# Four transformer layers on one core: row blocks of the sorted experts fetched in another order, a table part computed earlier, POOL drained twice more

## The chip, the core and the metric

The kernel is one program on one core of a Trainium2 chip. The core has five engines with instruction queues of their own: PE (TensorE, matmuls), DVE (VectorE), ACT (ScalarE), POOL (GpSimd) and SP (SyncE, which here only issues DMAs). They meet through semaphores. Times are device microseconds of one execution. Three executions of the kernel before took 1379.13, 1385.40 and 1386.09 us, median 1385.4 us. A fourth one was profiled.

## The reference

The input is `L0_attn_x`, 8 x 512 x 128 in fp32, which is 4096 tokens of 128 numbers. Four layers follow, each a pre-norm attention and a pre-norm feed-forward part:

```
x = L0_attn_x
x = x + _L0_attn_ref(_layernorm(x), ...)   # causal, no softmax, 16 heads of 8
x = x + _L0_ffn_ref(_layernorm(x), ...)    # one of 4 groups of 2 experts (128 -> 256 -> 128, silu gate)
x = x + _L1_attn_ref(_layernorm(x), ...)   # linear attention, elu + 1
x = x + _L1_ffn_ref(_layernorm(x), ...)    # one of 8 experts (128 -> 512 -> 128, relu), at most 512 tokens each
x = x + _L2_attn_ref(_layernorm(x), ...)   # sliding window of 64, softmax
x = x + _L2_ffn_ref(_layernorm(x), ...)    # dense, 128 -> 384 -> 128, int weights
x = x + _L3_attn_ref(_layernorm(x), ...)   # latent attention with rope, pages
x = x + _L3_ffn_ref(_layernorm(x), ...)    # one of 8 experts (128 -> 512 -> 128, exact gelu), no limit
return x
```

What matters here is that layers 0 and 3 route each token to one expert (group) by an argmax, and that the number of tokens of an expert is known only at run time. In layer 3:

```
expert_idx = jnp.argmax(router_probs, axis=-1)
h = jax.nn.gelu(x_flat @ w1[e] + b1[e], approximate=False)
y = h @ w2[e] + b2[e]
out = out + jnp.where(sel, expert_w, 0.0)[:, None] * y
```

## The kernel before, in words

The activations stay in SBUF (`X`, 32 tiles of 128 tokens). The program has six stretches, with a barrier of all five engines between any two. A barrier is a semaphore `bar` that every engine raises once; PE, DVE, ACT and SP raise it with a DRAIN instruction, POOL with a small memset of `mark` (line 2037), and each then waits for five more. Inside a stretch the order of each engine's work is fixed beforehand: by `lanes` from tables of due times (`ORDER0`, `ORDER2`) or written out by hand (`ORDER1`).

The first stretch is the attention and the routing of layer 0. While it runs, POOL scatters every token with an indirect DMA (line 2101) into a DRAM table `xs0`, sorted by expert: expert g owns 4096 rows. At its end DVE computes from the counts (`tables0`) a table `row_at` of 19 slots: for each slot the row of `xs0` at which 256 tokens of one expert begin, and the row of the weights. Then comes the barrier, and after it the first sorted expert stage: a slot s is fetched by SP (`fetch_x`, 132 KB, and `fetch_w`, 768 KB, into rings of four buffers), turned on PE (`g0_turn`, line 755), copied by ACT, multiplied up (`g0_up`, lines 767 and 768), activated, multiplied down (line 780), and POOL scatters the result back (`put`, line 2127). `g0_turn(1)` waits until ACT has copied the result of `g0_turn(0)`, and `g0_up(0)` stands behind both turns in PE's queue.

The row numbers are loaded by SP into a register (`slot_row`, a TENSOR_LOAD at line 2206), some register instructions make an address of it, and only then the DMA is issued (line 2218 for rows, 2212 for weights). The first weights are fetched ahead of the barrier (`grouped_ahead`), the first rows may not be: the last tokens are scattered just before it. `W_NEXT` says which weights follow which rows: in layer 0 the weights of slot s + 1 stand behind the rows of slot s, for s below 3.

Layer 3 has the same form with 23 slots of 256 or 128 tokens (`PLAN3`): three pairs of slots that share their weights, ten slots of 256 and seven of 128. Its table is made in parts by `tables3(level)`: level 4 ahead of the barrier (the first three pairs), level 2 behind it, and level 1 after the first rows have been turned. Each part raises `tab`, for which SP waits before it uses a row number of that part. DVE also copies the turned rows (line 1721), in the same queue as the table. In this stage POOL's `put` adds the result to `out` in DRAM with an indirect DMA (line 2127): one for each 128 tokens, so 39 for the 23 slots. POOL issues 205 indirect DMAs in the whole program (96 + 38 + 32 + 39). After the last it waits until all have landed, and the program's end follows, where every engine executes one more DRAIN (line 2331).

PE ends the first stretch with `warm(8)`, eight matmuls whose result nobody reads, then raises its barrier, and runs `warm(4)` behind it; the stretch before the last stage does the same with `warm(6)`.

The lines that decide most of it:

```
def barrier():                                   # SP's, line 2182
    S.drain().then_inc(sem["bar"], 1)
    e.wait_ge(sem["bar"], 5 * bars)

def fetch(L, s):                                 # line 2230
    if s > 3:
        e.wait_ge(sem["g_tok"], SLOT0[L] + s - 3)
    fetch_x(L, s)
    if L == 3 and s in TAB3:
        e.wait_ge(sem["tab"], TAB3[s])
    for n in W_NEXT[L].get(s, []):
        fetch_w(L, n)
```

Of the kernel before, what the change touches and what calls it, by code (L numbers as in the profile page):

```python
# [131 lines left out]
TILES3, COL3, WNUM3 = plan3()  # L132
SLOTS = {0: 19, 3: len(TILES3)}
# [5 lines left out]

W_NEXT = {0: {s: [s + 1 if s < 3 else s] for s in range(SLOTS[0]) if s != 3}, 3: {1: [1], 2: [2], 3: [3]}}  # L140
for n in range(4, len(PLAN3)):
    W_NEXT[3].setdefault(max(last_use3(n - 4) + 4, 4), []).append(n)
TAB3 = {1: 3, 2: 4}
# [218 lines left out]
def build(nc, inp, out):  # L362
    with ExitStack() as ctx:
# [217 lines left out]
        def pe_program(e):  # L581
# [9 lines left out]
            def warm(n):  # L591
                for _ in range(n):
                    PE.matmul(ps[:, 7, :], ident, W[:, 0:512], start=True, stop=True, skip_group_check=True)
# [152 lines left out]
            e.wait_ge(drained_of(last[:2], last[2]), after(last[:2], last[2]))  # L746
            warm(8)
            barrier()
# [340 lines left out]
        def dve_program(e):  # L1089
# [258 lines left out]
            def tables3(level):  # L1348
# [51 lines left out]
                if level == 4:  # L1400
# [19 lines left out]
                    choose(0, FOURS, 512)  # L1420
                if level == 2:
                    own.end(V.scalar_tensor_tensor(out=got, in0=take, scalar=512.0, in1=base, op0=ALU.mult, op1=ALU.add))
                    own.end(V.tensor_tensor(out=odd, in0=til, in1=full, op=ALU.subtract))
                    own.end(V.scalar_tensor_tensor(out=four, in0=take, scalar=-2.0, in1=full, op0=ALU.mult, op1=ALU.add))
                    settled()
                    limited(four, PAIRS)
                    scan(f(504), odd)
                    settled()
# [223 lines left out]
            for name, b in ORDER2["DVE"]:  # L1652
# [53 lines left out]
                elif name[:2] == "l3":  # L1706
                    tail(3, name, b)
            tables3(4)
            barrier()
            tables3(2)  # L1710
# [318 lines left out]
        def pool_program(e):  # L2029
# [140 lines left out]
            ysb3 = gviews(3)[4]  # L2170
            e.wait_ge(sem["out_done"], 16 * (B + 3))
            for s in range(SLOTS[3]):
                put(SLOT0[3] + s, s % 4, out, ysb3[s % 4], ALU.add, TILES3[s])
            for s in range(SLOTS[3], SLOTS[3] + 4):
# [3 lines left out]
        def sp_program(e):  # L2178
            e = Seat(e)
            bars = 0  # L2180

            def barrier():
                nonlocal bars
                bars += 1
                S.drain().then_inc(sem["bar"], 1)
                e.wait_ge(sem["bar"], 5 * bars)

            def stack(key, l):
# [24 lines left out]

            def fetch_x(L, s):
                k, E = s % 4, 4 if L == 0 else 8
                u = 2 if L == 0 else TILES3[s]
                rows = xs[L][bass.ds(slot_row(0, s if L == 0 else COL3[s], E * 4096), 128 * u), :].rearrange("(p u) d -> p u d", u=u)
                S.dma_start(gviews(L)[2][k][:, 0:u, :], rows).then_inc(gx[k], 16)
# [47 lines left out]
            e.wait_ge(sem["y1_rows"], 48)  # L2266
            barrier()
            for name, b in ORDER1["SP"]:
                if name == "g0_f":
                    fetch(0, b)  # L2270
                elif name == "f2":
                    S.dma_start(f2.bitcast(I32), inp["l2_ffn"]).then_inc(sem["f2_in"], 16)
                elif name == "l1_get":
                    due = min(2 * (b + 1) + 3, SLOTS[0])
                    for k in range(4):
                        e.wait_ge(y_out[k], 32 * len(range(k, due, 4)))
                    e.wait_ge(sem["mixed"], b)
                    S.dma_start(yg1, ys[0][1 + T * b:1 + T * b + T, :].rearrange("(t p) d -> p t d", p=128)).then_inc(sem["y0_in"], 16)
                elif name == "w1":
                    e.wait_ge(sem["g_down"], SLOTS[0])  # L2280
                    S.dma_start(MW[:, 512 * b:512 * b + 512], inp["l1_moe"][:, 512 * b:512 * b + 512]).then_inc(sem["w1_in"], 16)
# [44 lines left out]
            grouped_ahead(3)  # L2326
            barrier()
            for s in range(SLOTS[3]):
                fetch(3, s)
# [142 lines left out]
```

## Time and profile before

| what | value |
|---|---|
| three executions | 1379.13, 1385.40, 1386.09 us (median 1385.4) |
| profiled execution, its own time | 1376.14 us |
| its span (first to last instruction) | 1374.2 us |
| busy in the span: PE, DVE, ACT, POOL | 1102.5, 823.4, 568.4, 446.0 us |
| mean granted clock of PE | 0.927 |
| barrier ahead of the first sorted stage | about 202.4 us |
| barrier ahead of the last sorted stage | about 1270.4 us |
| last busy instruction of any compute engine ends | about 1365.9 us |

The profiled execution's own time is 1.9 us above its span. A row of the trace names an engine, the line of the kernel, the tile that it writes and those that it reads, and how often it stands there. A name with a q (SPq, POOLq, PEldq) is the engine's own instruction queue: register, semaphore, drain and DMA-issuing instructions, which count as no busy time. In a timeline, brackets give how long the engine had been idle before the instruction and who ended that.

### The profile page before, as it was taken

How to read it: one execution, taken by the hardware profiler on the slowest of the kernel's cores; microseconds unless marked ns; L12 is line 12 of the kernel's file. 1: busy time of each engine (PE TensorE's matmuls, PEld its weight loads, DVE VectorE, ACT ScalarE, POOL GpSimd, SP SyncE). 2: the span in 40 equal slices, each digit the busy share in tenths (PEclk: the TensorE clock that was granted, in tenths of full speed). 3: DMA queues.
4: the chain of work that ended last, by engine and by line, in shares of the span. 5: the costliest groups of instructions: out<-in, count | busy, mean ns of one | idle time of the engine just before them, and what ended most of it. 6: DMA issues, size and time to landing. Idle time of an engine off the chain costs nothing.

```text
span 1374.2 us, 39349 instructions
## 1 busy us (share of the span) xinstructions
PE 1102.5 (80%) x16861; PEld 803.4 (58%) x16861; DVE 823.4 (60%) x2399; ACT 568.4 (41%) x993; POOL 446.0 (32%) x538
## 2 busy tenths in 40 slices
PE   6999968888976794676788988888888887766895
PEld 4777747777864473443455655656565564443784
DVE  7577765568875122346748587686848575734432
ACT  3322103455451231314374654737374552551342
POOL 3223331344564154113122223133321403112475
PEclk9999979999996997788999999999999999877998
DMA  9454415543040511212211211212221100200784
GB/s 363 166 204 187 178 59 182 169 140 116 25 160 22 121 51 51 52 48 55 54 51 50 67 50 37 63 46 58 60 58 49 48 25 11 55 18 27 192 212 91
DMA packets 85167, 126.15 MB, mean 92 GB/s; under 512 B 14465, under 2 KB 66178, under 8 KB 84578
## 3 DMA queue, kind: packets, MB, share of 16 engines
q1 hardware_dynamic: 68258, 106.57, 24.6%
q0 software_dynamic: 10928, 13.64, 4.1%
q10 hardware_dynamic: 5808, 3.43, 0.9%
q8 instruction: 132, 2.16, 0.7%
q14 instruction: 41, 0.34, 0.1%
HBM read 50.92 MB, written 46.74 MB: 71 GB/s over the span
## 4 chain that ended last, share of the span: by engine, by line
PE 38%; DVE 26%; ACT 10%; issue 10%; POOL 7%; DMA 5%; SPq 1%; another core or an unknown queue 1%; PEldq 1%; ACTq 1%; DVEq 0%; PEld 0%; POOLq 0%
DVE mx L1680 10%; ACT MW L1963 5%; DVE mx L1671 2%; DVE bst L1112 2%; PE ps L873 2%; PE ps L1033 2%; PE ps L976 2%; PE ps L858 2%; PE ps L780 2%; PE ps L967 2%; POOL xs L2101 2%; PE ps L889 2%; PE ps L767 1%; PE ps L768 1%; DVE X L1140 1%
## 5 line engine op out<-in xcount | busy, mean ns | idle before, releaser
L1680 DVE TENSOR_REDUCE mx<-ps 128x2 f32<-128x1024 f32 (+3 forms) x176 | 188.4, 1119 | 33.2 <-PE ps L1006 33.0
L1963 ACT ACTIVATE MW<-ps 128x1024 f32<-128x1024 f32 x160 | 154.6, 1029 | 75.9 <-PE ps L1018 62.9
L2101 POOL DMA_INDIRECT xs<-xr,sidu x96 | 96.2, 1002 | 138.8 <-DVE sidu L1271 101.3
L2044 POOL TENSOR_SCALAR rst<-bmv 128x4 f32<-128x4 f32 x64 | 15.8, 246 | 286.6 <-DVE bmv L1115 285.9
L1033 PE MATMUL ps<-MW,Vp 128*16 128x128 f32 x2560 | 88.2, 279 | 3.7 <-ACT MW L1963 3.5
L1006 PE MATMUL ps<-K,Q 64*128 64x512 bf16 (+3 forms) x512 | 61.6, 315 | 22.9 <-DVE mx L1680 16.9
L1950 ACT ACTIVATE MW<-ps 128x1024 f32<-128x1024 f32 x64 | 63.6, 1030 | 25.3 <-PE ps L938 23.3
L601 PE MATMUL ps<-W,xr 128*128 128x128 f32 x192 | 36.6, 323 | 45.5 <-DVE xr L1125 32.5
L1033 PEld LDWEIGHTS ps<-MW,Vp 128*16 128x16 f32 x2560 | 64.1, 98 | 15.2 <-ACT MW L1963 4.6
L2127 POOL DMA_INDIRECT out_dram<-qf,toku x39 | 60.6, 1555 | 34.9 <-DVE toku L1736 26.7
L1769 ACT COPY XT<-ps 128x512 f32<-128x512 f32 x48 | 28.2, 588 | 101.2 <-PE ps L601 83.2
L1671 DVE TENSOR_REDUCE mx<-ps 128x8 f32<-128x768 f32 x64 | 57.9, 949 | 18.7 <-PE ps L915 16.3
L1018 PE MATMUL ps<-Q,K 64*128 64x128 bf16 x1280 | 58.9, 222 | 9.9 <-DMA Q<-mT 3.9
L2023 ACT ACTIVATE MW<-ps,MW 128x256 f32<-128x256 f32 (+1 forms) x92 | 34.0, 439 | 60.3 <-PE ps L1078 58.1
L1018 PEld LDWEIGHTS ps<-Q,K 64*128 64x128 bf16 x1280 | 39.0, 96 | 31.2 <-issue 12.2
L601 PEld LDWEIGHTS ps<-W,xr 128*128 128x128 f32 x192 | 25.8, 168 | 52.3 <-issue 32.1
L1112 DVE BATCH_NORM_STATS2 bst<-X 128x6 f32<-128x128 f32 x256 | 55.4, 278 | 1.2
L2127 POOL DMA_INDIRECT ys<-xp,toku x38 | 37.6, 990 | 55.7 <-DVE toku L1524 46.9
L1006 PEld LDWEIGHTS ps<-K,Q 64*128 64x128 bf16 x512 | 19.2, 95 | 55.0 <-DVE mx L1680 26.4
L634 PE MATMUL ps<-W,tmpA 128*128 128x128 f32 x256 | 41.0, 288 | 12.8 <-DVE mx L1680 4.4
L2047 POOL TENSOR_TENSOR rst<-rst,npow 128x4 f32<-128x4 f32 x48 | 49.8, 1038 | 4.0
L1140 DVE TENSOR_TENSOR X<-ps,X 128x512 f32<-128x512 f32 x40 | 27.6, 690 | 36.4 <-PE ps L739 10.7
(373 smaller groups left out, 2675.2 us busy)
## 6 DMA issues: line engine op xcount, KB each, us to landing
xs<-hb SPq DMA_DIRECT2D x52, 528.0 KB, 9.1
MW<-l_moe_dram SPq DMA_DIRECT2D x19, 768.0 KB
MW<-l_moe_dram SPq DMA_DIRECT2D x20, 578.0 KB
Q<-spl SPq DMA_DIRECT2D x48, 128.0 KB
Q<-spm SPq DMA_DIRECT2D x48, 128.0 KB
K<-spl SPq DMA_DIRECT2D x43, 128.0 KB
K<-spm SPq DMA_DIRECT2D x43, 128.0 KB
MW<-l_moe_dram SPq DMA_DIRECT2D x16, 256.0 KB
```

Source lines behind the costliest of these rows:

```text
L601: m = PE.transpose(p[:, 128 * t:128 * t + 128], xr_of(key)[:, t, 0:128], ident)
L1006: m = PE.matmul(p[:, o:o + nk], Q3[i][64 * k:64 * k + 64, s, 128 * t:nk], K3[i][64 * k:64 * k + 64, s, 0:nk], start=True, stop=True, tile_ ...
L1018: m = PE.matmul(p[:, o:o + 128], K3[i][64 * k:64 * k + 64, 4 * half + s, 128 * kt:128 * kt + 128], Q3[i][64 * k:64 * k + 64, 4 * half + s, ...
L1033: m = PE.matmul(ps[32 * j:32 * j + 16, 7, 128 * g:128 * g + 128], Vp[1][:, 4 * i + kt, h, :], P3[k % 2][:, col(h)[0] + 128 * col(h)[1]:col ...
L1112: own.end(V.bn_stats(out=bst[:, k, t, :], in_=X[:, 4 * b + t, :]))
L1671: V.tensor_reduce(out=mx[0][:, :, 4 * half:4 * half + 4, t], in_=p.rearrange("p (e n) -> p e n", e=2)[:, :, 0:384].rearrange("p e (s k) -> ...
L1680: V.tensor_reduce(out=mx[1][:, :, s0:s0 + ns, t], in_=p.rearrange("p (e n) -> p e n", e=2)[:, :, 0:ns * nk].rearrange("p e (s k) -> p e s ...
L1950: A.activation(P2[t % 2][:, 1024 * half:1024 * half + 1024], p, ACT.Exp).then_inc(drained[u], 1)
L1963: A.activation(P3[k % 2][:, 1024 * half:1024 * half + 1024], p, ACT.Exp).then_inc(drained[u], 1)
L2047: G.tensor_tensor(out=rst[:, k, 1, :], in0=rst[:, k, 0, :], in1=npow[:, :], op=ALU.pow).then_inc(rstd_on[k], 1)
L2101: G.indirect_dma_start(out=xs[L], out_offset=bass.IndirectOffsetOnAxis(ap=sidu[:, 4 * b + t:4 * b + t + 1], axis=0), in_=src[:, t, :], in_ ...
L2127: G.indirect_dma_start(out=dst, out_offset=at, in_=y[:, v, :], in_offset=None, compute_op=how).then_inc(y_out[k], 16)
```

## The change

Four things are changed.

First, SP at the two barriers. The barrier is split into `arrive` (the DRAIN) and `passed` (the wait). Between the two SP loads the row numbers of slots 0 and 1 into registers. Behind the barrier it issues the rows of slots 0 and 1, and after them the weights of slot 1. In layer 0 these weights used to stand between the two row blocks; in layer 3 the two row blocks already stood first, but each with its own load ahead of it.

Second, DVE: the first thirteen instructions of the old level 2 (through `limited(four, PAIRS)`) are now `tables3(3)` and stand ahead of the barrier. The rest of level 2 stays behind it.

Third, PE: `warm(8)` becomes `warm(6)` at the end of the first stretch.

Fourth, POOL: a DRAIN stands ahead of the 23 puts of the last stage, and another one ahead of the put of slot 11. By then POOL has issued 166 indirect DMAs before the first DRAIN, 19 more before the second, and 20 follow.

```
-W_NEXT = {0: {s: [s + 1 if s < 3 else s] for s in range(SLOTS[0]) if s != 3}, 3: {1: [1], 2: [2], 3: [3]}}
+W_NEXT = {0: {s: [s] for s in range(4, SLOTS[0])}, 3: {1: [1], 2: [2], 3: [3]}}
...
-            warm(8)
+            warm(6)
             barrier()
             warm(4)
...
-                if level == 2:
+                if level == 3:
                     own.end(V.scalar_tensor_tensor(out=got, in0=take, scalar=512.0, in1=base, op0=ALU.mult, op1=ALU.add))
                     own.end(V.tensor_tensor(out=odd, in0=til, in1=full, op=ALU.subtract))
                     own.end(V.scalar_tensor_tensor(out=four, in0=take, scalar=-2.0, in1=full, op0=ALU.mult, op1=ALU.add))
                     settled()
                     limited(four, PAIRS)
+                if level == 2:
                     scan(f(504), odd)
...
             tables3(4)
+            tables3(3)
             barrier()
             tables3(2)
...
             e.wait_ge(sem["out_done"], 16 * (B + 3))
+            G.drain()
             for s in range(SLOTS[3]):
+                if s == SLOTS[3] // 2:
+                    G.drain()
                 put(SLOT0[3] + s, s % 4, out, ysb3[s % 4], ALU.add, TILES3[s])
...
-            def barrier():
+            def arrive():
                 nonlocal bars
                 bars += 1
                 S.drain().then_inc(sem["bar"], 1)
+
+            def passed():
                 e.wait_ge(sem["bar"], 5 * bars)
...
+            def x_row(L, s):
+                return slot_row(0, s if L == 0 else COL3[s], (4 if L == 0 else 8) * 4096)
...
-            barrier()
+            arrive()
+            first = [x_row(0, s) for s in range(2)]
+            passed()
+            for s in range(2):
+                fetch_x(0, s, first[s])
+            fetch_w(0, 1)
+            for s in (2, 3):
+                fetch_x(0, s)
+                fetch_w(0, s)
             for name, b in ORDER1["SP"]:
                 if name == "g0_f":
-                    fetch(0, b)
+                    if b > 3:
+                        fetch(0, b)
...
             grouped_ahead(3)
-            barrier()
-            for s in range(SLOTS[3]):
+            arrive()
+            first = [x_row(3, s) for s in range(2)]
+            passed()
+            for s in range(2):
+                fetch_x(3, s, first[s])
+            e.wait_ge(sem["tab"], TAB3[1])
+            fetch_w(3, 1)
+            for s in range(2, SLOTS[3]):
                 fetch(3, s)
```

The order of SP's instructions at the first sorted stage, before. `MW` is the weights' ring, `tco` the rows' ring, a TENSOR_LOAD fetches one number of `row_at`, an ISA row is register work. The barrier stands between the first DMA and the load behind it; drains and waits are not shown.

```order
L2212 DMA MW<-l0_moe_dram 128x1536
L2206 TENSOR_LOAD row_at
L2218 ISA
L2218 DMA tco<-xs0 128x264
L2206 TENSOR_LOAD row_at
L2212 ISA
L2212 DMA MW<-l0_moe_dram 128x1536
L2206 TENSOR_LOAD row_at
L2218 ISA
L2218 DMA tco<-xs0 128x264
```

And the same place now:

```order
L2223 DMA MW<-l0_moe_dram 128x1536
L2217 TENSOR_LOAD row_at x2
L2233 ISA
L2233 DMA tco<-xs0 128x264
L2233 ISA
L2233 DMA tco<-xs0 128x264
L2217 TENSOR_LOAD row_at
L2223 ISA
L2223 DMA MW<-l0_moe_dram 128x1536
```

The second row block has moved from behind the weights of slot 1 to before them, and both of the first loads now stand directly behind the first weights.

PE's queue around the first barrier, as the difference of the two programs:

```order
 L626 MATMUL ps<-hota,W 128x16
-L593 MATMUL ps<-W 128x512 x12
+L593 MATMUL ps<-W 128x512 x10
 L755 MATMUL ps<-W,tco 128x128 x4
```

Only the two unread matmuls are gone (eight and four before, six and four now); the turns of the first rows follow as before. DVE's instructions have the same order in both programs; what moves there is the place of the barrier among them.

## Rows read from the trace of the kernel before

**Rows 1.** Busy time by window: the last sorted stage (us, engines, PEclk, DMA share, GB/s)

```profile
1272.00:1366.00 94.00, 79.31 (x540) 70.26 (x539) 35.41 (x156) 33.99 (x92) 60.64 (x39) 0.99 0.75 178
```

**Rows 2.** Instructions of line 2331, the program's end (ns min/median/max, first and last start)

```profile
L2331 POOLq COMPARE_BRANCH  x1: 41/41/41, 1367.6 to 1367.6; - x1
L2331 POOLq DRAIN  x1: 6196/6196/6196, 1367.8 to 1367.8; - x1
```

**Rows 3.** DMA traffic from 1367.8 us to the end

```profile
DMA packets 0, 0.00 MB, mean 0 GB/s; under 512 B 0, under 2 KB 0, under 8 KB 0
```

**Rows 4.** Instructions of line 2462, the program's start

```profile
L2462 POOLq DRAIN  x1: 169/169/169, 0.3 to 0.3; - x1
```

**Rows 5.** Groups by line: POOL's indirect DMAs (count, busy us, mean ns, idle before)

```profile
L2101 POOL DMA_INDIRECT xs<-xr,sidu x96 | 96.2, 1002 | 138.8 <-DVE sidu L1271 101.3 <-issue 24.4 <-DVE sidu L1265 13.1
...
L2127 POOL DMA_INDIRECT out_dram<-qf,toku x39 | 60.6, 1555 | 34.9 <-DVE toku L1736 26.7 <-issue 8.2
...
L2127 POOL DMA_INDIRECT ys<-xp,toku x38 | 37.6, 990 | 55.7 <-DVE toku L1524 46.9 <-issue 8.9
...
L2145 POOL DMA_INDIRECT ys<-qf,gidu x32 | 30.6, 958 | 49.3 <-DVE qf L1612 41.6 <-issue 7.6
```

**Rows 6.** Timeline of POOL, last stage (start, us, line, operation, idle before and releaser)

```profile
1284.99 1.62 POOL L2127 DMA_INDIRECT out_dram<-qf,toku  x1 [14.61 <-DVE toku L1736]
...
1324.23 1.55 POOL L2127 DMA_INDIRECT out_dram<-qf,toku  x1 [1.41 <-DVE toku L1736]
...
1335.65 1.55 POOL L2127 DMA_INDIRECT out_dram<-qf,toku  x1 [2.21 <-DVE toku L1736]
...
1356.93 1.55 POOL L2127 DMA_INDIRECT out_dram<-qf,toku  x1 [2.46 <-DVE toku L1736]
...
1364.36 1.55 POOL L2127 DMA_INDIRECT out_dram<-qf,toku  x1 [0.30 <-issue]
```

**Rows 7.** Chain that ended last, around the first sorted stage's barrier (start, us, what)

```profile
193.33 9.02 PEldq L588
202.37 0.28 SPq L2206
```

**Rows 8.** Waits of SP's queue (total us, times, longest)

```profile
SPq L2206 <- PEq L588: 0.5, 1, 0.5
```

**Rows 9.** Timeline of all engines, start of the first sorted stage

```profile
201.28 0.36 SPq L2212 DMA_DIRECT2D MW<-l_moe_dram  x1
...
202.81 0.35 SPq L2218 DMA_DIRECT2D tco<-xs  x1
...
204.43 0.33 SPq L2218 DMA_DIRECT2D tco<-xs  x1
...
206.76 0.44 PE L755 MATMUL ps<-W,tco 128*128 128x128 f32 x2 [0.67 <-DMA tco<-xs]
...
207.30 0.37 ACT L1839 COPY tco<-ps 128x256 f32<-128x256 f32 x1 [18.41 <-PE ps L755]
...
209.48 0.44 PE L755 MATMUL ps<-W,tco 128*128 128x128 f32 x2 [2.28 <-DMA tco<-xs]
```

**Rows 10.** Busy time by window: the first transfers of that stage

```profile
202.00:205.25 3.25, 3.17 (x8) 1.42 (x8) 1.98 (x5) 0.00 (x0) 0.00 (x0) 1.00 0.87 289
202.00:208.20 6.20, 4.46 (x11) 1.65 (x10) 1.98 (x5) 0.37 (x1) 0.00 (x0) 1.00 0.89 300
```

**Rows 11.** Timeline of all engines, start of the last sorted stage

```profile
1268.66 0.17 DVE L1382 TENSOR_SCALAR row_at<-tab 128x3 int32<-128x3 f32 x1
...
1270.42 0.17 DVE L1422 SCALAR_TENSOR_TENSOR rt<-rt 128x8 f32<-128x8 f32 x1 [1.59 <-POOL mark L2037]
...
1271.61 0.17 DVE L1386 TENSOR_TENSOR_SCAN rt<-rt 128x8 f32<-128x8 f32 x1
...
1274.08 0.44 PE L1054 MATMUL ps<-W,tmpA 128*128 128x128 f32 x2
...
1275.48 0.42 DVE L1721 COPY tmpA<-ps 128x256 f32<-128x256 f32 x1
```

More of the change, by code:

```diff
@@ L2185, in barrier @@
                 S.drain().then_inc(sem["bar"], 1)
+            def passed():
                 e.wait_ge(sem["bar"], 5 * bars)
+            def barrier():
+                arrive()
+                passed()
             def stack(key, l):
@@ L2212, in fetch_w, with fetch_x @@
                 S.dma_start(gviews(L)[0][k], src[bass.ds(slot_row(1, s if L == 0 else COL3[WNUM3.index(s)], 128 * E - 128), 128), :]).then_inc(gw[k], 16)
-            def fetch_x(L, s):
-                k, E = s % 4, 4 if L == 0 else 8
+            def x_row(L, s):
+                return slot_row(0, s if L == 0 else COL3[s], (4 if L == 0 else 8) * 4096)
+            def fetch_x(L, s, row=None):
+                k = s % 4
                 u = 2 if L == 0 else TILES3[s]
-                rows = xs[L][bass.ds(slot_row(0, s if L == 0 else COL3[s], E * 4096), 128 * u), :].rearrange("(p u) d -> p u d", u=u)
+                row = x_row(L, s) if row is None else row
+                rows = xs[L][bass.ds(row, 128 * u), :].rearrange("(p u) d -> p u d", u=u)
                 S.dma_start(gviews(L)[2][k][:, 0:u, :], rows).then_inc(gx[k], 16)
@@ L2326, in sp_program @@
             grouped_ahead(3)
-            barrier()
-            for s in range(SLOTS[3]):
+            arrive()
+            first = [x_row(3, s) for s in range(2)]
+            passed()
+            for s in range(2):
[3 more added lines that the diff above has]
+            for s in range(2, SLOTS[3]):
                 fetch(3, s)
```

## The prediction

> **What bounds the kernel now.** I read the views in the order end, stage, start. The end first: the last POOL instruction starts at 1364.36 and takes 1.55 us [rows 6], so all compute is over at 1365.91, but the span ends at 1374.2. Of these 8.3 us the instructions of the program's last line show where they go: POOL's queue passes its waits for the last landings by 1367.65, and then a single DRAIN of POOL takes 6.196 us [rows 2]. In those 6.2 us no DMA packet moves at all [rows 3]. So the last 0.45% of the time is one queue instruction that shows in no list of busy groups. The only other DRAIN of POOL stands at the start, when it has issued no DMA, and takes 0.169 us [rows 4]. Between the two POOL has issued 96 + 39 + 38 + 32 = 205 indirect DMAs [rows 5].
>
> Then the stage ahead of the end. POOL's puts run at 1.55 us with 0.30 between them, but the reader is to see in the timeline that POOL waits for DVE's `toku` again and again, the last time 2.46 us before the final five [rows 6]. So the stage is paced by the chain PE, DVE, SP and the weights' DMA, not by POOL; a late POOL in the middle is caught up.
>
> Then the two starts. At the first barrier the chain goes through PE's own queue, 9.02 us of drain behind the unread matmuls, and then to SP's load [rows 7]; yet SP waited only 0.5 us for PE [rows 8]. Behind it PE turns the first rows at 206.76 and the second only at 209.48, after 2.28 us of waiting for `tco`, and the first product stands behind that turn [rows 9]. At the last stage's barrier DVE sits idle 1.59 us until POOL's mark, then computes the table from 1270.42 on, and copies the turned rows at 1275.48 although PE had turned them from 1274.08 to 1274.52 [rows 11]. There DVE's table is the bound, not the rows.
>
> Everything between the two places is a chain of waits of one engine for another that starts from the first barrier, with nothing tied to the clock on the wall. So time gained at 202 us is carried to the end.
>
> **The last DRAIN.** Taken as a fixed 0.169 us plus an equal share for each DMA issued since the last DRAIN, 6.196 - 0.169 over 205 is 29.4 ns each. With a DRAIN at 166 and one at 185, the last one finds 20: 0.169 + 20 x 0.0294 = 0.76 us. Saving 5.4 us. The bounds: nothing saved if the time has nothing to do with the count, 6.0 us if it falls to the 0.169 us of the start. I take 5.4, since the two DRAINs in the trace differ in just this, the DMAs issued before them, and no transfer was left to wait for.
>
> The Trainium skill speaks against it: "VectorE: DVE Perf Modes", section "The DRAIN you can't avoid", says that the DRAINs of preamble and postamble cost a constant of about 12 ns on all five engines. By that rule the sum would be the 2.65 us of the starts alone. The trace differs, 6196 ns for POOL's last one.
>
> **The DRAIN ahead of the puts.** By the same rate 166 DMAs cost 0.169 + 4.9 = 5.1 us. It starts when the barrier opens at 1270.4, and POOL has nothing to do until 1284.99, an idle time of 14.61 us [rows 6]. It costs nothing up to 14 us, with the old 6.2 us too.
>
> **The DRAIN at slot 11.** Nineteen DMAs of the stage stand before it, the 20th is the one at 1324.23 [rows 6]. The DRAIN has to wait until the 19th has landed: from the end of the last DMA's issue to the end of POOL's waits is 1367.65 - 1365.91 = 1.7 us, and 0.169 + 19 x 0.0294 = 0.7 us come behind it. That is 2.4 us, of which the idle 1.41 less the usual 0.30 covers 1.1. The 20th put is 1.3 us late at most. The gaps at 1335.65 and 1356.93 give back 2.21 + 2.46 - 0.60 = 4.07 us, so nothing is left of it at the end. What queues behind it is only POOL's own puts; DVE needs their output buffers again four slots later, some 10 us on. Cost 0; bounds 0 and, if this DRAIN took the whole 6.2 us behind the landing, 1.7 + 6.2 - 1.1 - 4.07 = 2.7 us.
>
> **First sorted stage.** SP arrives at the barrier at 202.37 - 0.5 = 201.87. Taking away two of PE's eight unread matmuls from a piece of 9.02 us shortens it by more than 0.5 us even at twice the mean pace, so the barrier opens with SP at about 201.9; no more than 0.5 us can come from it. SP's two loads take 0.28 each [rows 7] with about 0.03 between, register work 0.15, so the rows of slot 0 are issued at about 202.6 instead of 202.81, those of slot 1 at about 203.0 instead of 204.43. But the rows of slot 0 do not come sooner: they stand behind 768 KB of weights issued at 201.28, and from 202.00 to 205.25 at 289 GB/s 0.94 MB moved, which is just these weights and the 132 KB [rows 10]. The turn of slot 1 waited for 1.86 MB (6.2 us at 300 GB/s: two weights and two row blocks [rows 10]), done at 208.2, and PE started 1.3 us later. Now it waits for 1.06 MB, done at about 205.7, there at about 207.0. The next limit is late at once: `g0_turn(1)` also waits for ACT's copy, which ends at 207.67 [rows 9]. So it starts at 207.7 instead of 209.48: 1.8 us. Bounds: 0 if the transfers share the engines and slot 1's rows come no sooner; 2.3 if slot 0's rows too come by the 0.5 us of the barrier. The second weights are issued at about 203.8 instead of 203.6, and by the measured rate are done at 208.2 and usable at 209.5; only if `g0_up(0)`, which starts at 208.1, took less than 1.4 us for its eight products of 128 x 256 would PE wait for them.
>
> The removed unread matmuls leave PE idle for about 1.3 us at the barrier. The granted clock stays at 1.00 until 208.2 [rows 10], well into the 2.28 us of idle before 209.48 [rows 9], which is the 2.4 GHz level, so I charge nothing.
>
> **Last sorted stage.** The thirteen moved instructions take from 1270.42 to 1271.61, 1.19 us [rows 11]. DVE's last instruction before the barrier ends at 1268.83 and it then idles 1.59 us, so they fit with 0.4 us to spare, less DVE's own DRAIN. The table then ends 1.19 us sooner, at 1274.3 instead of 1275.5, but the copy now has to wait for PE's turn, over at 1274.52. It starts at about 1274.6 instead of 1275.48: 0.88 us. SP's two loads begin only when it arrives, close to the barrier itself, so its rows are 0.1 us later at worst. I take 0.85 us; bounds 0 and 1.19. The second copy stands behind the rest of the table, as before, and keeps the shift.
>
> The skill has a figure against this: "DMA: Bandwidth & Descriptors", section "Latency and other measured facts", gives a TENSOR_LOAD a floor of about 600 ns. Two of them would put the rows 0.6 us later, and this stage would keep 0.2 us. Row 202.37 shows 0.28 us.
>
> **Sum.** 5.4 + 1.8 + 0.85 = 8.05 us. Against the profiled execution's own 1376.14 us that is 1368.1. The median of the three runs is 9.3 us above that execution, so the same saving stands against 1385.4: 1377.3 us, forecast 1377.
>
> **Rivals.**
> Not shortened: the last DRAIN keeps its 6.2 us, because it is a fixed price of a POOL that has issued indirect DMAs. Then each added one costs the same. The one at slot 11 leaves 2.7 us at the end, and 2.65 come from the starts: 0.05 us in all, 1385 us. For it: there is only one long DRAIN, so no rate can be read from it. Against: nothing that POOL or the DMAs do is left at 1367.8.
>
> Starts given back: slot 1's rows come no sooner, or PE falls to its lower clock at the first barrier, and only 5.4 + 0.85 = 6.25 us remain: 1379 us. For it: the transfers stand at 0.87 to 0.89 of all engines [rows 10]. Against: the row blocks of slot 0 did come when 0.94 MB had moved.
>
> Slower: the DRAIN at slot 11 waits for a moment in which no DMA at all is in flight, SP's weights too. They keep the DMA engines at a share of 0.75 through the stage [rows 1], and stop only when DVE stops, in slot 15, because the buffers of slot 11 are not free, so that SP's last fetch is the one released by slot 14, whose put is at 1335.65 [rows 6]: near 1336.5. With 3.3 us for the last weights (592 KB at this stage's 178 GB/s) the DRAIN ends near 1340, and the 20th put is 16 us late; less 4.07 that is 12 us at the end, against 8.05 gained: 4 us slower, 1389 us. It decides from a hold of POOL of 8.05 + 4.07 = 12.1 us on. Against: the last DRAIN ran 6.2 us with nothing in flight, so it wasn't packets that it waited for.
>
> **Chances.** Forecast 0.73, not shortened 0.14, starts given back 0.09, slower 0.04. About 0.5% or 6.9 us is what a measurement of this kernel can tell from no change; the three runs themselves lie 7 us apart. The forecast's 8.05 is only 1.1 us above that line, and medians of runs that spread like this move by some 2 to 3 us, so I give it two chances in three of showing as faster, the third case one in three: 0.73 x 0.67 + 0.09 x 0.33 = 0.52, rounded up to 0.54 for a last DRAIN nearer 0.2 us. The slower case shows as slower about half the time, and a few per cent come from the scatter: 0.05. The rest, 0.41, is within 0.5%. The forecast's own range is 1370 to 1382, from the lowest of the three runs less 8 and the highest less 4; with the first rival it reaches to 1385. I give 1369 to 1385.
>
> **What would show it.** POOL's DRAIN at the end of the program at 0.8 us instead of 6.2, and the two new ones at about 5 and 2.4 us (5 too short means that the count isn't the price; 6 twice, the first rival). The put that follows the second one at most 1.3 us late, and the last gap of POOL still there. The turn of slot 1 about 5.8 us after the barrier instead of 7.1, released by ACT and not by the DMA. The copy of line 1721 4.2 us after the last stage's barrier instead of 5.06. I am wrong if the last DRAIN is still above 3 us, or if a DMA wait stands where ACT's should.

## The result and the profile after

The changed kernel takes 1375.14 us (median of 19 runs, 1365.98 to 1380.99), the kernel before 1382.26 us (19 runs, 1376.74 to 1393.5). The ratio is 0.9938, 95% interval [0.992, 0.9956]: about 8.6 us or 0.62% faster, and by the interval 6.1 to 11.1 us. The two medians themselves lie 7.1 us apart. Forecast were 1377 us and 8.05 us.

The two profiled executions don't show this. That of the changed kernel took 1377.76 us and the one shown of before 1376.14. The reason stands in the busy times by stretch (columns: window, length, busy us of PE, PEld, DVE, ACT and POOL with their counts, granted clock, DMA share, GB/s). Of before:

```profile
202.00:450.00 248.00, 203.13 (x1135) 170.81 (x1135) 165.36 (x565) 104.53 (x232) 107.13 (x143) 0.92 0.36 118
530.00:1270.00 740.00, 579.60 (x11564) 384.47 (x11564) 465.27 (x1097) 357.75 (x554) 182.69 (x241) 0.92 0.18 47
```

And of the changed kernel:

```profile
202.00:450.00 248.00, 205.17 (x1132) 172.46 (x1132) 165.63 (x565) 104.43 (x232) 107.40 (x142) 0.90 0.37 118
530.00:1275.00 745.00, 589.17 (x11565) 388.15 (x11566) 466.59 (x1107) 357.53 (x554) 183.21 (x242) 0.90 0.18 47
```

DVE, ACT and POOL are busy as long as before. PE has the same matmuls and is busy some 10 us longer in the long stage, because TensorE's granted clock is 0.90 there and not 0.92. The lower clock comes in stretches at half speed (1.2 GHz), here 3.4 us long, which fall at other places in every execution:

```profile
270.00:275.50 5.50, 3.08 (x20) 2.39 (x19) 5.28 (x16) 4.05 (x11) 2.35 (x4) 1.00 0.00 0
275.50:278.90 3.40, 3.40 (x12) 2.78 (x11) 0.00 (x0) 0.86 (x2) 2.90 (x3) 0.50 0.15 43
```

In the changed kernel's 19 runs time and mean clock go together (correlation -0.87, 6.8 us for 0.01 of clock), which is most of their spread of 15 us. So the terms are read below as distances inside the traces: from POOL's last mark to the end, from a barrier to the first copy. The medians tell the sum.

**The end.** Instructions of the program's last line (queue, operation, ns), the answer to [rows 2]:

```profile
L2361 POOLq COMPARE_BRANCH  x1: 46/46/46, 1373.9 to 1373.9; - x1
L2361 POOLq DRAIN  x1: 1680/1680/1680, 1374.1 to 1374.1; - x1
```

The DRAIN went from 6196 to 1680 ns: 4.5 us saved. The two added ones:

```profile
L2174 POOLq DRAIN  x1: 8077/8077/8077, 1274.8 to 1274.8; - x1
L2177 POOLq DRAIN  x1: 7912/7912/7912, 1326.0 to 1326.0; - x1
```

The first lies in POOL's idle time. Of the second the record begins while two puts ahead of it are still being issued; what it costs shows in POOL's timeline, the answer to [rows 6]:

```profile
1316.81 1.55 POOL L2129 DMA_INDIRECT out_dram<-qf,toku  x1 [4.92 <-DVE toku L1738]
...
1334.59 1.55 POOL L2129 DMA_INDIRECT out_dram<-qf,toku  x1 [5.08 <-DVE toku L1738]
...
1351.32 1.55 POOL L2129 DMA_INDIRECT out_dram<-qf,toku  x1 [0.30 <-DVE toku L1738]
...
1362.87 1.55 POOL L2129 DMA_INDIRECT out_dram<-qf,toku  x1 [0.69 <-DVE toku L1738]
...
1370.30 1.55 POOL L2129 DMA_INDIRECT out_dram<-qf,toku  x1 [0.30 <-issue]
```

The 20th put waits 5.08 us where it waited 1.41. The profile names `toku`, but DVE had written it long before: the DRAIN ends at 1326.0 + 7.9 = 1333.9, 0.7 us ahead of the put. Behind it every gap is gone, and of the last one, 2.46 us before, 0.69 is left. Not all of that is the DRAIN's: the 4.92 us ahead of the 13th put come earlier, in a stretch at half clock (35 to 38 us behind POOL's last mark), and put 19 already starts 53.3 us behind the mark instead of 51.0.

**First sorted stage**, the answer to [rows 9]:

```profile
202.45 1.03 DVE L1529 MEMSET spl<- 128x516 f32 x2 [1.51 <-SPq L2190]
203.09 0.86 SPq L2233 DMA_DIRECT2D tco<-xs  x2
206.60 0.45 PE L755 MATMUL ps<-W,tco 128*128 128x128 f32 x2 [0.57 <-DMA tco<-xs]
207.14 0.37 ACT L1841 COPY tco<-ps 128x256 f32<-128x256 f32 x1 [17.80 <-PE ps L755]
207.66 0.41 PE L755 MATMUL ps<-W,tco 128*128 128x128 f32 x2 [0.61 <-ACT tco L1841]
```

The second turn now waits for ACT, at 207.66 instead of 209.48. SP is the last to arrive (`<-SPq L2190`). The two numbers come from two executions, and DVE's last table instruction (line 1346) starts at 200.76 in this one and at 200.31 in that of before. Counted from it, the second turn comes 6.90 us later instead of 9.17, so 2.27 us sooner. In the traces of the experiments below this distance is 8.80 to 9.64 us in the four other kernels with the old order and 6.74 to 7.02 in seven of the eight others with the new one (7.78 in the eighth, `end_ladder`, where PE falls to half clock just there).

**Last sorted stage**, the answer to [rows 11]:

```profile
1274.83 0.18 DVE L1386 TENSOR_TENSOR_SCAN rt<-rt 128x8 f32<-128x8 f32 x1 [0.22 <-SPq L2190]
1275.63 0.88 SPq L2233 DMA_DIRECT2D tmpA<-xs  x2
1279.11 0.44 PE L1054 MATMUL ps<-W,tmpA 128*128 128x128 f32 x2 [0.56 <-DMA tmpA<-xs]
1279.58 0.42 DVE L1723 COPY tmpA<-ps 128x256 f32<-128x256 f32 x1 [0.79 <-PE ps L1054]
```

DVE goes straight on with the last part of the table, and its copy stands 4.75 us behind the barrier instead of 5.06. It now waits 0.79 us for PE's turn, which waits for the rows, issued 0.80 us behind the opening (before: 1270.87 - 1270.42 = 0.45 us).

### The profile page after: what moved, and what is told of

It is laid out like the page before. It is cut to its first block, busy times and chain, and to the rows that moved or that the text cites. A ratio compares the mean times of both kernels' runs of the same rounds, so it can differ in the third digit from the quotient of the medians.

```text
span 1376.0 us, 39343 instructions
## 1 busy us (share of the span) xinstructions
PE 1116.8 (81%) x16857; PEld 811.4 (59%) x16857; DVE 824.1 (60%) x2399; ACT 568.2 (41%) x993; POOL 447.0 (32%) x538
## 4 chain that ended last, share of the span: by engine, by line
PE 40%; DVE 25%; ACT 11%; issue 10%; POOL 7%; DMA 5%; SPq 1%; another core or an unknown queue 1%; ACTq 1%; DVEq 0%; POOLq 0%
DVE mx L1681 10%; ACT MW L1965 5%; PE ps L873 2%; PE ps L967 2%; DVE bst L1112 2%; PE ps L976 2%; DVE mx L1672 2%; PE ps L858 2%; PE ps L1033 2%; PE ps L767 2%; PE ps L780 2%; PE ps L889 2%; PE ps L768 2%; PE ps L968 2%; PE ps L1064 1%
## 5 line engine op out<-in xcount | busy, mean ns | idle before, releaser
L2103 POOL DMA_INDIRECT xs<-xr,sidu x96 | 96.0, 1000 | 138.7 <-DVE sidu L1271 101.3
L767 PE MATMUL ps<-tco,MW 128*128 128x256 f32 x152 | 46.8, 390 | 2.9 <-ACT tco L1841 1.3
```

Of the source, the lines that this page charges most:

```text
L767: PE.matmul(p[:, 256 * jj:256 * jj + 256], wt_[:, 128 * j:128 * j + 128], xsT0[s % 2], start=True, stop=True)
L2103: G.indirect_dma_start(out=xs[L], out_offset=bass.IndirectOffsetOnAxis(ap=sidu[:, 4 * b + t:4 * b + t + 1], axis=0), in_=src[:, t, :], in_ ...
```

## The experiments

**Which part gives what.** Four kernels, timed beside the kernel before (29 runs, median 1385.88; 12 runs of each, 6 of first_only):

```
no_drains    both G.drain() of the changed kernel left out
first_only   if s == SLOTS[3] // 2: G.drain()              left out
mid_only     G.drain() ahead of the loop over the slots    left out
drains_only  the kernel before, with the two G.drain()
```

> The changed kernel without its two new DRAINs of POOL. Theory C (a DRAIN's price grows with the indirect DMAs issued since the last one): the DRAIN at the program's end is back at 6.2 us (205 DMAs behind it), POOL's gap ahead of the 20th put back at 1.1 to 2 us. The time is 4.5 us above the changed kernel's, about 0.2% under the kernel before (what the two starts give: 1.8 us at the first sorted stage, 0.3 at the last). Rival F (the end became shorter for another reason, the earlier starts or the place of the waits): the last DRAIN stays at 1.7 us. The first sorted stage's second turn starts 5.3 to 5.4 us after the barrier in both.

> The changed kernel with the DRAIN ahead of the puts, without the one at slot 11. Theory C, from the two last DRAINs seen (205 DMAs: 6.196 us, 20 DMAs: 1.680 us, so 24 ns a DMA and 1.2 us fixed): 39 DMAs give a last DRAIN of 2.1 us, 0.45 us more than with both. POOL's gap ahead of the 20th put falls from 5.1 to 1 to 2 us, and POOL's last gap grows from 0.7 to 2 or 2.5. Since POOL was 0.4 us from bounding the end, the time is the changed kernel's plus 0.5 us, within what can be measured. Rival (the DRAIN at slot 11 costs what it saves or more): not slower than the changed kernel, or 1 us faster.

> The changed kernel with the DRAIN at slot 11, without the one ahead of the puts. Theory C: the DRAIN at slot 11 now has 185 DMAs behind it instead of 19. At the 24 ns of the last DRAINs it takes 4.1 us longer than the 2.5 us that it took behind the landing of the 19th, at the 48 ns of the first one (8.08 us for 166) 8 us longer; the last DRAIN stays at 1.7 us. The 20th put is 8 to 12 us late instead of 4, POOL bounds the rest of the stage, and the end is 3 to 7 us later than in the changed kernel, about as before. Rival F (a DRAIN costs a fixed 6 to 8 us whatever was issued): the DRAIN at slot 11 as long as in the changed kernel, no change in time.

> The kernel before with only the two new DRAINs. Theory C: the last DRAIN at 1.7 us, 4.5 us less than 6.2; 4.5 us faster than the kernel before (0.3%), if the starts carry the rest of the measured 8.6 us. Rival (the DRAINs bring it all and the starts are lost on the way to the end): as fast as the changed kernel, 0.6% under the kernel before.

Measured (POOL's last mark is its last MEMSET ahead of the last stage's barrier; put 20 is the first behind slot 11's DRAIN):

| kernel | median us | ratio [95%] | last DRAIN us | idle ahead of put 20 | mark to end of span |
|---|---|---|---|---|---|
| before | | 1 | 6.20 | 1.41 | 103.9 |
| changed | | 0.9938 [0.992, 0.9956] | 1.68 | 5.08 | 101.3 |
| no_drains | 1382.48 | 0.9971 [0.9946, 0.9996] | 6.20 | 1.89 | 105.0 |
| first_only | 1376.21 | 0.9927 [0.99, 0.9955] | 3.23 | 1.56 | 99.5 |
| mid_only | 1380.2 | 0.9946 [0.9922, 0.9969] | 1.69 | 6.48 | 99.1 |
| drains_only | 1381.26 | 0.9966 [0.9943, 0.9989] | 1.68 | 5.14 | 103.2 |

The last column is from single traces and moves by 1 to 2 us with the clock (the changed kernel's and that of drains_only hold a half-clock stretch of 3.4 us in the middle of the stage). Three things follow. The DRAINs alone give about 0.34% (4.7 us) and the starts alone about 0.29% (4.0 us), and the two add up to what the whole change gives; the intervals (some 1.5 to 8 and 0.6 to 7.5 us) are too wide to order them. The last DRAIN's time hangs on what POOL issued since the one before it: with the first DRAIN alone, 39 puts before the end:

```profile
L2359 POOLq DRAIN  x1: 3231/3231/3231, 1368.1 to 1368.1; - x1
```

That is 3.23 us (2.1 expected), above the 1.3 us of 29.4 ns for each, and the whole 6.20 is back in no_drains. So neither my rate nor a fixed price holds. And slot 11's DRAIN buys 1.55 us at the end (3.23 to 1.68) for some 3.5 us in the middle (5.08 against 1.56): by the times first_only can't be told from the changed kernel. With slot 11's alone the put behind it waits 1.4 us more than in the changed kernel, though 185 indirect DMAs stand before it and not 19. I had expected its put 8 to 12 us late; it is 5.1 us late:

```profile
1328.01 1.55 POOL L2129 DMA_INDIRECT out_dram<-qf,toku  x1 [0.30 <-issue]
1336.03 1.55 POOL L2129 DMA_INDIRECT out_dram<-qf,toku  x1 [6.48 <-issue]
```

**What a DRAIN of POOL costs.** One execution each of four kernels; their times (1379.86, 1380.78, 1386.08 and 1386.87 us) lie within the spread and decide nothing. `ladder` is the kernel before with `G.drain()` behind each of POOL's four later barriers, and one more as its last instruction:

```
+            G.drain()      (behind barriers 2, 3, 4 and 5: 32, 70, 32, 32 indirect DMAs)
             for s in range(SLOTS[3], SLOTS[3] + 4):
                 e.wait_ge(y_out[s % 4], put3(s))
+            G.drain()
```

> The kernel before with a DRAIN of POOL behind each of its four later barriers (behind the 32 scatters of the first layer, the 38 puts and 32 scatters of the second stage, the 32 expert puts of the third, the 32 scatters of the last one) and one more at the end, behind the last wait for the puts, so that the compiler's own DRAIN follows with nothing issued in between. Theory P (a price per indirect DMA issued since the last DRAIN, some 80 ns of it, flattened for long stretches by something unknown): about 2.6, 5.6, 2.6, 2.6 us at the barriers, 3.2 us for the DRAIN added at the end (39 puts behind it, as in the kernel with the first DRAIN alone), and under 0.3 us for the compiler's. Theory K (the price hangs on the kind: a put that accumulates costs 83 ns, a scatter or plain put about 18 ns): 0.6, 1.3, 0.6, 0.6 us at the barriers and 3.2 us at the end. Theory F (a fixed price of about 6 us in the first DRAINs): each of the early ones 5 to 8 us, and the compiler's at the end over 1 us though nothing lies behind it.

```profile
L2122 POOLq DRAIN  x1: 2682/2682/2682, 202.2 to 202.2; - x1
L2142 POOLq DRAIN  x1: 5759/5759/5759, 451.0 to 451.0; - x1
L2152 POOLq DRAIN  x1: 2651/2651/2651, 530.7 to 530.7; - x1
L2173 POOLq DRAIN  x1: 2651/2651/2651, 1278.3 to 1278.3; - x1
L2180 POOLq DRAIN  x1: 3222/3222/3222, 1374.5 to 1374.5; - x1
L2336 POOLq DRAIN  x1: 46/46/46, 1377.8 to 1377.8; - x1
```

Theory P holds, and sharper than stated: 46 ns with nothing behind, 2651 for 32, 3222 for 39, 5759 for 70. From the first and the third, (3222 - 46) / 39 = 81.4 ns each; 70 then give 5.75. Scatters, plain puts and adding puts cost alike, so theory K falls, and the 46 ns end theory F.

`end_ladder` is the changed kernel with one more DRAIN, four row blocks from the end:

```
-                if s == SLOTS[3] // 2:
+                if s in (SLOTS[3] // 2, SLOTS[3] - 4):
```

> The changed kernel with one DRAIN of POOL more, four row blocks from the end. Theory P and theory K both give about 83 ns for each put behind the last DRAIN: with some 7 or 8 puts behind it the compiler's DRAIN takes 0.6 to 0.7 us instead of 1.68. A fixed part of 1.2 us, as the first estimate with its 29.4 ns per DMA would need, gives 1.4 us. The added DRAIN itself waits for the put in flight (about 2 us) and costs 12 or 13 puts of 83 ns, 1.1 us; with only 0.39 us of POOL's idle time left ahead of the end, nearly all of it comes out behind the last mark: the puts end 2.5 to 3.5 us later and the span grows by 1.5 to 3 us at an equal clock.

```profile
L2361 POOLq DRAIN  x1: 537/537/537, 1378.2 to 1378.2; - x1
```

Six puts stand behind the added one, 46 + 6 x 81.4 = 534 ns; measured 537. The put behind it waits 3.02 us:

```profile
1365.23 1.56 POOL L2129 DMA_INDIRECT out_dram<-qf,toku  x1 [3.02 <-issue]
```

From mark to end of the span it is 103.2 us, 1.9 more than in the changed kernel, inside what was expected (both traces hold a half-clock stretch at the same place, 35 to 39 us behind the mark).

Then longer counts, each the kernel before with one DRAIN, behind POOL's third barrier (`one_102`) or its fourth (`one_134`):

```
             for k in range(2):
                 e.wait_ge(scat[k], 64 * B)          (one_134: m_out[k], 64 * (NEXP // 2))
             barrier()
+            G.drain()
```

> The kernel before with one DRAIN more, behind POOL's third barrier: 102 indirect DMAs stand before it and 103 between it and the end. Theory N (46 ns and 81.4 ns for each indirect DMA since the last DRAIN, at any count up to about 100): 8.35 us there and 8.43 us at the end, so the end gets 2.2 us longer than the 6.20 us of before, although fewer DMAs stand behind it. Theory R (N, and beyond 128 DMAs without a DRAIN some 65 of them are retired on the way without a price that shows): the same two numbers here. Rival C (the price flattens out smoothly with the count, 5.76 at 70, 8.08 at 166): both between 6 and 7.5 us.

> The kernel before with one DRAIN more, behind POOL's fourth barrier: 134 indirect DMAs stand before it and 71 between it and the end. The end, by all theories: 46 + 71 x 81.4 ns = 5.83 us. The one behind 134: theory N carried on, 10.95 us; theory R, 134 less 65, 5.6 to 5.8 us; rival C, 7 to 8 us.

Of one_102 (102 before the first, 103 before the last):

```profile
L2141 POOLq DRAIN  x1: 8403/8403/8403, 455.3 to 455.3; - x1
L2332 POOLq DRAIN  x1: 7314/7314/7314, 1376.7 to 1376.7; - x1
```

Of one_134 (134, and 71):

```profile
L2150 POOLq DRAIN  x1: 5463/5463/5463, 537.8 to 537.8; - x1
L2332 POOLq DRAIN  x1: 5849/5849/5849, 1378.7 to 1378.7; - x1
```

The line goes on to 102 (8.35 expected) and holds for 71 (5.83 expected). Beyond, it breaks: 134 cost less than 71, 166 cost 8.08, 205 cost 6.20, and 103 at the end 7.31. Theory R, that some 65 drop out on the way in a long stretch, is near for 134 (5.6 to 5.8 expected) and wrong for the 103 (8.43 expected). Divided by 81.4 ns, the price is short of about 67 DMAs at 134, of 67 at 166, of 129 at 205 and of 14 at the 103. No indirect DMA of POOL took longer than 1.62 us in the traces of before, the changed kernel, ladder, mid_only, one_102 or one_134, so I can't point at where they drop out. What makes the price fall at high counts stays open; up to 102, at nine different counts, it is 46 ns and 81 to 82 ns for each.

**First sorted stage: order or unread matmuls?** `warm8` is the changed kernel with

```
-            warm(6)
+            warm(8)
             barrier()
```

> The changed kernel with eight idle-time matmuls instead of six ahead of the barrier in front of the first sorted stage. Theory W (TensorE's queue holds the second turn of the stage back): the second turn starts at about 5.5 us after the barrier opens, 0.9 us or more later than with six (207.66 against a barrier at 202.28), and the first two copies of DVE lie 4.7 and about 7.5 us behind the barrier instead of 4.69 and 5.65. Rival L (the order of the loads alone did it): the second copy stays at 5.6 to 5.7 us behind the barrier.

```profile
204.04 0.36 SPq L2223 DMA_DIRECT2D MW<-l_moe_dram  x1
204.74 1.03 DVE L1529 MEMSET spl<- 128x516 f32 x2 [1.50 <-SPq L2190]
205.39 0.86 SPq L2233 DMA_DIRECT2D tco<-xs  x2
208.88 0.44 PE L755 MATMUL ps<-W,tco 128*128 128x128 f32 x2 [0.55 <-DMA tco<-xs]
209.93 0.41 PE L755 MATMUL ps<-W,tco 128*128 128x128 f32 x2 [0.61 <-ACT tco L1841]
```

From DVE's first instruction behind the barrier to the second turn it is 5.19 us, in the changed kernel 207.66 - 202.45 = 5.21. The rival has it for this distance: the second turn owes its gain behind the barrier to SP's loads (their order and the two register loads moved ahead; no run parts these) and not to the two matmuls.

The distance begins at the opening, though, and can't show what the matmuls do to the opening itself. Of before:

```profile
202.51 1.03 DVE L1528 MEMSET spl<- 128x516 f32 x2 [2.03 <-PEq L588]
```

SP had issued its last weights at 201.28, so DVE goes on 1.23 us behind that, released by PE. The same distance is 1.24 us in ladder, 1.06 in one_134 and 2.03 in drains_only, PE the last each time. It is 0.70 or 0.71 us, SP the last, in all eight traces with six matmuls, and also in one_102 and warm8, which have eight. So with eight of them PE held the barrier back by 0.36 to 1.33 us in four traces of six, and with six in none of eight. That the two matmuls did it is the reading that fits; warm8's one trace happens to be one in which SP came last.

**Last sorted stage.** `table_back` is first_only with

```
-            tables3(3)
             barrier()
+            tables3(3)
```

> The changed kernel without the DRAIN at slot 11 and with the moved part of the last table back behind DVE's arrival at the last barrier. Theory T (DVE's table is what the first copy of the last stage waits for, and the move took 1.19 us of it away): the copy comes 5.1 to 5.3 us behind POOL's mark, as before, instead of 4.48, and PE's turn lies ready before it. Rival (the row load was the bound in both kernels): the copy stays at 4.5 to 4.9 us.

```profile
1271.96 0.10 POOL L2039 MEMSET mark<- 128x1 f32 x1 [1.41 <-DMA xs<-xr,sidu]
1275.99 0.45 PE L1054 MATMUL ps<-W,tmpA 128*128 128x128 f32 x2
1277.17 0.42 DVE L1723 COPY tmpA<-ps 128x256 f32<-128x256 f32 x1
```

The copy stands 5.21 us behind the mark and PE's turn was over 0.7 us earlier: DVE's table is the bound again. Of first_only:

```profile
1272.06 0.10 POOL L2039 MEMSET mark<- 128x1 f32 x1 [1.42 <-DMA xs<-xr,sidu]
1276.54 0.42 DVE L1723 COPY tmpA<-ps 128x256 f32<-128x256 f32 x1 [0.37 <-PE ps L1054]
```

4.48 us, and it waits for PE. So the move is worth 0.73 us there. What bounds the copy then is PE's turn (1276.06), behind the rows and, by 0.13 us, behind PE's unread matmuls. Over all traces the copy stands 5.19 to 5.22 us behind the mark in the six kernels with the old table and 4.40 to 4.91 in the eight with the moved one. (The time of table_back's single execution, 1374.37 us, says nothing here.)

`early` tries to bring the rows sooner. It is first_only with SP's arrival ahead of its wait for the tables:

```
+                    arrive()
                 e.wait_ge(sem["tab"], 1 if L == 0 else 2)
                 fetch_w(L, 0)
...
-            arrive()
             first = [x_row(3, s) for s in range(2)]
```

> The changed kernel without the DRAIN at slot 11, and with SP's arrival at the last barrier moved ahead of its wait for the tables and of the first weights' load, so that the row registers are loaded before the barrier opens. Theory S (SP is the last to arrive, by 0.1 us, and its register loads delay the first rows): the first row load is issued 0.1 to 0.3 us behind the opening instead of 0.80, the first copy of the stage comes 4.0 to 4.3 us behind POOL's mark instead of 4.5 to 4.9, and the stage ends up to 0.5 us earlier; the ratio is then 0.9915 to 0.993 where the kernel with the first DRAIN alone had 0.9927 [0.99, 0.9955], not to be told from it by the times. Rival (the tables are the last thing SP waits for, and that wait now comes after the opening): the first row load still goes 0.7 us or more behind the opening and nothing moves.

```profile
1275.78 0.10 POOL L2039 MEMSET mark<- 128x1 f32 x1 [1.52 <-DMA xs<-xr,sidu]
1275.93 3.70 PE L593 MATMUL ps<-W 128*128 128x512 f32 x8 [0.40 <-POOL mark L2039]
1276.43 0.88 SPq L2231 DMA_DIRECT2D tmpA<-xs  x2
1279.70 0.44 PE L1054 MATMUL ps<-W,tmpA 128*128 128x128 f32 x2
1280.18 0.42 DVE L1723 COPY tmpA<-ps 128x256 f32<-128x256 f32 x1 [0.33 <-PE ps L1054]
```

The barrier now opens with POOL, not with SP, and the rows go 0.65 us behind the mark (0.94 in first_only). The turn gains only 0.08 of it (3.92 against 4.00): PE's unread matmuls end at 1275.93 + 3.70 = 1279.63, 0.07 us ahead of it, so they are the next limit. The ratio was 0.9949 [0.9915, 0.9983], above the 0.9915 to 0.993 expected: no gain that can be told.

**A version that uses the law.** `two_gaps` is the changed kernel with two DRAINs at slots where POOL waited anyway:

```
-                if s == SLOTS[3] // 2:
+                if s in (4, 14):
```

> The changed kernel with its DRAIN at slot 11 replaced by two, ahead of the puts of slot 4 (7 puts since the last DRAIN) and of slot 14 (17 more), where POOL waited 0.97 and 1.91 us longer than the usual 0.30 in the kernel before; 15 puts are left for the end. By 46 ns and 81.4 ns for each: the last DRAIN takes 1.27 us. The two cost the landing of the last put (1.2 to 2.8 us) and 0.62 and 1.43 us behind it and 0.42 us until the next put starts, so 2.2 to 3.8 and 3.1 to 4.7 us, less the gaps: 1.3 to 2.9 us late after slot 4, all of it taken back by the gaps of 1.8 and 1.1 us at slots 7 and 11; 1.2 to 2.8 us late after slot 14, of which the gaps at slots 18 and 20 give back 2.6. Theory G (gaps absorb what is short enough): the last put ends 94 to 96 us behind POOL's last mark, as without any such DRAIN, and the time is 0.4 us below the changed kernel's and 2.0 us below that with the first DRAIN alone; ratio 0.991 to 0.993. Rival (a wait for the landing costs 4 us wherever it stands, as at slot 11): 97 us or more behind the mark, and a ratio of 0.993 to 0.995.

```profile
L2361 POOLq DRAIN  x1: 1272/1272/1272, 1371.5 to 1371.5; - x1
```

```profile
1305.74 1.55 POOL L2129 DMA_INDIRECT out_dram<-qf,toku  x1 [4.95 <-issue]
...
1342.06 1.55 POOL L2129 DMA_INDIRECT out_dram<-qf,toku  x1 [5.05 <-DVE toku L1738]
...
1368.09 1.55 POOL L2129 DMA_INDIRECT out_dram<-qf,toku  x1 [0.30 <-issue]
```

The last DRAIN takes 1.27 us as worked out. Each of the two holds POOL for about 5 us, more than the 2.2 to 3.8 and, by 0.3 us, the 3.1 to 4.7 expected: 7 puts cost as much as 17 or 19, though 46 ns and 81.4 ns each make 0.62 us of 7 and 1.59 of 19. Taking this off, and 0.69 us from the DRAIN's end to the next put as at slot 11, leaves 2.8 to 3.6 us for the landing of the put in flight, an estimate, so the landing is most of it (the rival is right on that). Theory G is right on the outcome: the last put ends 95.1 us behind the mark, among the kernels without such a DRAIN (95.6 in before, 94.0 in first_only), and mark to end is 98.5 us, the shortest seen. Median 1376.7 (6 runs), ratio 0.9926 [0.9898, 0.9954]; this can't be told from 0.9927 of first_only or from the changed kernel's. With POOL's last gap gone (0.30) there is no room for a third.

## Why the prediction was right

The time (1377 against 1375.14) and the sum (8.05 against about 8.6 us) held, and luck has a part in both. The 1377 is counted from the median of three runs, 1385.4, which lies 3.1 us above that of the 19. And the terms as the traces show them, below, give 4.5 + 1.8 to 2.3 + 0.3 to 0.7 us, less 0 to 1.4 for slot 11: 5.2 to 7.5 us and not 8.6. So the last DRAIN was put 0.9 us too high, and a remainder that no trace locates made up for it. Part of it may be the clock: its mean is 0.918 over the changed kernel's 19 runs and 0.9165 over the 55 runs of the kernel before whose clock is on record, and at 6.8 us for 0.01 that would be some 1 us (an estimate). The rest stays open.

- **The last DRAIN**: the mechanism was right, the size was off. The term failed in the step "a fixed 0.169 us plus an equal share for each": the 205 DMAs of before lie where price and count no longer go together. Measured are 46 ns and 81.4 ns each, so 1.68 us are left and not 0.76; saved were 4.5 us, predicted 5.4. "The two DRAINs in the trace differ in just this" gave one difference, from which no rate follows, and was not quite so: with nothing issued the one at the start takes 169 ns and the last one of ladder 46. The Trainium skill ("VectorE: DVE Perf Modes", section "The DRAIN you can't avoid"), which has a constant of about 12 ns, comes near only with nothing behind the DRAIN (46 ns here).
- **The DRAIN ahead of the puts**: hidden, as said; 8.1 us and not 5.1, in an idle time of 13.8.
- **The DRAIN at slot 11**: predicted was a put at most 1.3 us late; it was 3.7 us late (5.08 against 1.41). Too small were the landing, 1.7 us as read at the end of the program, where it was about 2.8 here (5.08 less 1.59 for 19 DMAs and 0.69 until the put, an estimate), and the share of the 19, 0.7. The bound that I had worked out for the worst case, 1.7 + 6.2 of DRAIN, held. The cost at the end was put at 0 with a slack of 4.07. In the changed kernel's trace most of that slack is gone (2.46 to 0.69), but 2.3 us of the lateness came before the DRAIN, with the half-clock stretch; in warm8's trace, with the same DRAINs, 2.69 us of the last gap are left. mid_only has no such stretch and ends its last put 95.3 us behind the mark, 1.35 us later than first_only (94.0), but the eight traces without a DRAIN among the puts lie between 94.0 and 96.5. So the term is 0 to about 1.4 us, and no run tells it from 0.
- **First sorted stage**: 1.8 us at the second turn, released by ACT, as said; counted from DVE's last table instruction it is 2.3 us, the upper bound. "But the rows of slot 0 do not come sooner" did not hold: counted in this way PE's first turn starts 5.84 us and not 6.45 us behind the table. That goes with the opening of the barrier: in one_102, the old order with SP last, it is 5.84 us too. The barrier opened at 202.3 and not at 201.9 as worked out, but in this execution all of SP's work there lies 0.46 us later (its weights' load at 201.74 instead of 201.28). The unread matmuls made no difference behind the opening (warm8); ahead of it PE held the barrier up in four of six traces with eight of them and in none with six. I had allowed up to 0.5 us for this; it was 0.36 to 1.33.
- **Last sorted stage**: 0.85 us predicted, 0.73 by table_back against first_only, 0.3 in the changed kernel's own trace. "So its rows are 0.1 us later at worst" was the weak step: the rows were issued 0.80 us behind the opening where it had been 0.45, and PE's turn, not the table, set the copy.
- **Rivals**: "Not shortened" fell with 1.68 us and with no_drains, whose 6.20 came back. "Starts given back": the clock from 202 to 209 us stayed at 1.00 and the turn kept its gain; of the nine traces with the new order only end_ladder's has a half-clock stretch there, and its second turn is 0.9 us later. "Slower": the put behind the DRAIN at slot 11 was 3.7 us late and not 16. SP had issued weights at 1331.97, and in the last 1.4 us before the DRAIN ended the DMA engines had a share of 0.80 (142 GB/s), so it does not wait for other queues' traffic.

## What to carry to other kernels

Read the queue instructions of the last line: a wait that no busy list shows can be half a per cent. An instruction whose price depends on what was issued before it can be moved into an idle time and paid there, but only as far as the count behind it stays small; a second one in a busy stretch also pays for the landing of what is in flight. When the gain is smaller than the spread of the clock, compare distances inside the traces, and leave the sum to the medians.

## What the runs showed of the hardware

- POOL's DRAIN with no DMA in flight: 46 ns plus 81 to 82 ns for each indirect DMA issued since its last DRAIN, the same for scatters and adding puts, at 0, 6, 15, 20, 32, 39, 70, 71 and 102 of them. Above that 5.46 us (134), 8.08 (166), 6.20 (205), and 7.31 for 103 of one kernel; no rule found.
- A DRAIN behind a put in flight held POOL for 4.95 to 5.65 us with 7, 17 or 19 DMAs since the last one while SP loaded weights (six DRAINs at slots 4, 11 and 14, in five traces), for 6.48 us with 185, and for 3.02 us with 14 near the end, when the DMA engines' share fell to 0.05.
- TensorE's half-clock stretches (granted clock 0.50) fall at other places in each execution: in the last stage, leaving out the one that every trace has around and after the last puts, 35 to 38 us behind POOL's mark in the changed kernel's trace, 24 to 28 in drains_only, 36 to 39 in end_ladder, 69 to 72 in warm8 and nowhere in the other ten. 0.01 of mean clock goes with 6.8 us of this kernel.
